# Attention on one Trainium2 core: softmax denominators inverted by ScalarE's logarithm and exponential instead of VectorE's reciprocal

## The reference

```
scores = einsum('bqhd,bkhd->bhqk', q, k) / hd + slopes * rel      # causal, else the lowest float
attn   = softmax(scores, axis=-1)
out    = einsum('bhqk,bkhd->bqhd', attn, v).reshape(B, S, H)
return out @ w_proj + b_proj
```

## Time and profile before

| | us |
|---|---|
| median of 3 runs (lowest, highest) | 1267.71 (1266.81, 1270.55) |
| the profiled execution | 1269.12 |
| its span | 1267.3 |

### The profile page before, as it was taken

The page is one execution under the profiler, slowest core; times in us unless marked ns, Lnnn a source line. Parts: engine busy times, 40 slices in busy tenths (PEclk is TensorE's granted clock), DMA queues, the critical chain, the costliest instruction groups (busy, mean ns, idle before and its releaser), DMA issues. The chain is left out here.

```text
span 1267.3 us, 31645 instructions
## 1 busy us (share of the span) xinstructions
PE 1114.0 (88%) x12161; PEld 914.5 (72%) x12161; DVE 869.7 (69%) x2188; ACT 630.5 (50%) x1433; POOL 387.9 (31%) x561
## 2 busy tenths in 40 slices
PE   6569998779979995657799999999999999999987
PEld 5446776657778994546557888888888888888776
DVE  6466997778846678767476677667766776664574
ACT  4434555331433664547644554555455545553654
POOL 3331123076710155771055016202620261000120
PEclk9769999687989998777999999999999999999998
DMA  7737885222279886462343234223343332232001
GB/s 175 187 115 208 221 226 193 100 79 84 80 262 418 320 301 225 144 178 100 112 105 98 85 111 126 85 85 114 121 152 90 117 114 88 90 102 80 1 18 50
DMA packets 77986, 176.17 MB, mean 139 GB/s; under 512 B 12614, under 2 KB 26182, under 8 KB 75270
## 3 DMA queue, kind: packets, MB, share of 16 engines
q1 hardware_dynamic: 71564, 157.09, 38.8%
q0 software_dynamic: 6272, 17.05, 4.4%
HBM read 112.82 MB, written 61.08 MB: 137 GB/s over the span
## 5 line engine op out<-in xcount | busy, mean ns | idle before, releaser
L2373 ACT ACTIVATE decay<-masked,negcum 128x128 f32<-128x128 f32 x512 | 163.0, 391 | 102.1 <-DVE mixT L2437 102.1
L2281 PE MATMUL joint<-xh,w_high 128*128 128x512 f32 x512 | 209.3, 409 | 2.2 <-POOL wl L2217 2.2
L2281 PE MATMUL joint<-xl,w_high 128*128 128x512 f32 x512 | 200.2, 391 | 0.0
L2281 PE MATMUL joint<-xh,wl 128*128 128x512 f32 x512 | 199.8, 390 | 0.0
L2485 DVE COPY cT<-joint 128x512 f32<-128x512 f32 x128 | 88.3, 690 | 85.7 <-PE joint L2281 85.4
L2391 ACT ACTIVATE bT<-joint 128x512 f32<-128x512 f32 x128 | 76.7, 599 | 130.8 <-PE joint L2281 130.8
L2437 DVE TENSOR_TENSOR mixT<-pcb,decay 128x512 f32<-128x512 f32 x128 | 82.4, 685 | 55.8 <-PE pcb L2297 55.7
L2214 POOL TENSOR_TENSOR w_high<-w_in,none 128x512 fp32r<-128x512 f32 x32 | 35.0, 1094 | 261.4 <-DMA w_in<-in_w_bc 250.8
L2281 PEld LDWEIGHTS joint<-xh,w_high 128*128 128x128 f32 x512 | 96.1, 188 | 23.9 <-POOL wl L2217 2.6
L2281 PEld LDWEIGHTS joint<-xh,wl 128*128 128x128 f32 x512 | 96.1, 188 | 20.7
L2281 PEld LDWEIGHTS joint<-xl,w_high 128*128 128x128 f32 x512 | 96.3, 188 | 17.0
(11 more groups left out here) (367 smaller groups left out, 2711.7 us busy)
## 6 DMA issues: line engine op xcount, KB each, us to landing
cumrow<-ssm_cum SPq DMA_DIRECT2D x128, 256.0 KB, 3.3
slots_in<-blank SPq DMA_DIRECT2D x16, 1024.0 KB, 5.5
rows<-slots_in SPq DMA_DIRECT2D x32, 512.0 KB, 5.3
slots_out<-spare SPq DMA_DIRECT2D x32, 512.0 KB, 3.9
weights<-in_expert_quads SPq DMA_DIRECT2D x16, 768.0 KB, 9.1
w_in<-in_w_bc SPq DMA_DIRECT2D x32, 256.0 KB, 3.7
qk_parts<-parts SPq DMA_DIRECT2D x32, 192.0 KB, 2.3
stack<-qk_parts SPq DMA_DIRECT2D x32, 192.0 KB, 5.3
```

Source lines behind the costliest of these rows:

```text
L2281: last = nc.tensor.matmul(bank[:], w[:, j, col:col + P], a[:, k, c * CHUNK:(c + 1) * CHUNK], start=(m == 0), stop=(m == len(parts) - 1))
L2373: last = nc.scalar.activation(decay[:, n % 2, o], masked[:, n % 2, o], ACT.Exp, bias=negcum[:, c * TPC + i, head:head + 1])
```

## The change

DVE's two reciprocals per unit go. ACT gets a function `invert` that takes the natural logarithm of the denominators (128x256, from PSUM to SBUF) and then the exponential of its negative in place, with a semaphore (`logged`) between the two. DVE's `normalise` waits for ACT's one signal in place of its own two.

```
@@ stage_attention
-        inverted, normed = chip.sem("inverted"), chip.sem("normed")
+        logged, inverted, normed = chip.sem("logged"), chip.sem("inverted"), chip.sem("normed")
@@ block.scalar
+                def invert(u):
+                    act.wait_ge(pv_done, u + 1)
+                    if u:
+                        act.wait_ge(normed, u)
+                    nc.scalar.activation(rinv[:], po[u % 2][:, 1, :], ACT.Ln).then_inc(logged, 1)
+                    act.wait_ge(logged, u + 1)
+                    nc.scalar.activation(rinv[:], rinv[:], ACT.Exp, scale=-1.0).then_inc(inverted, 1)
...
                         hand_over(n // HALF - 1)
+                    u = i // HALF - 2
+                    if i % HALF == AT_BLOCK and 0 <= u < UNITS:
+                        invert(u)
@@ block.vector
-                def invert(u, half):
-                    if half == 0:
-                        dve.wait_ge(pv_done, u + 1)
-                        if u:
-                            dve.wait_ge(normed, u)
-                    cols = slice(half * P, (half + 1) * P)
-                    nc.vector.reciprocal(rinv[:, cols], po[u % 2][:, 1, cols]).then_inc(inverted, 1)
-
                 def normalise(u):
-                    dve.wait_ge(inverted, 2 * u + 2)
+                    dve.wait_ge(inverted, u + 1)
...
-                        for half in range(2):
-                            invert(u, half)
                         normalise(u)
                         block_norms(u + 2)
```

## The result

The changed kernel took 1284.01 us (median of 4 runs, 1282.55 to 1285.83) against 1267.61 us for the kernel before: a ratio of 1.0138 [1.0111, 1.0164]. By the medians that is 16.4 us slower, by the ratio (which is not the quotient of the medians) 17.5 us. The forecast was 1282 us. The profiled execution of the changed kernel took 1282.55 us, span 1280.7 us.

The account below looks back on a forecast made before the run. No engine is busy throughout attention; what is late when a window ends (DVE's or ACT's path) counts. Windows 12.5 us plus one clock loss gave 14.2 us on 1267.7: 1282 us, range 1264.5 to 1291.

Parts of the forecast that it names:

- The load back to the exponential: On ACT in the attention stage: returning from logarithm to exponential needs another table load, taken as 1.28 us.
- one table serves both: Rival: ACT loads once, each inversion takes 0.88 us; net -1.6 us, 1266 us, no measurable change; chance 0.24.
- the 1.8 us at the end: In the one-table rival, the last projection of the attention stage starts 1.8 us earlier.
- The inversion of 3.48 us: Each inversion on ACT: two loads of 1.28 us, two activations of 0.42 us, four gaps of 0.02 us.
- The windows: Attention's per-unit stretches, w0 onward, from one unit's `values` to the next: late inversions lengthen them by 12.5 us in all.
- Whose path: Which engine delays the next window: DVE's late maxima in w4, w6, w10; ACT's queued scalings and exponentials in w8, w12.
- The clock: PE's granted clock falls after the longer stalls behind w8 and w12; one loss of 1.7 us counted for both.
- the rival of six falls: Late windows idle PE 1 to 2 us more; six clock losses of 1.7 us, 23 us, 1290 us; chance 0.10.
- ACT's waits for turned scores: In attention, ACT's waits for PE's turned scores shrink by some 40 us as inversions fill them.
- The end: Last two inversions on ACT end about 227.4 us, where the last reciprocal ended at 227.47: nothing gained or lost.

Follow-up runs that it names:

- loads_aside: Kernel before, DVE still inverting, plus a logarithm and exponential of a scratch tile with their loads on ACT in each window, nobody waiting: 1279.66 us, 1.0091.
- clock_fill_fit: Changed kernel plus long f32 matmuls of no use on PE in w4, w6, w8, w10 and w12, sized to fit its waits: 1278.72 us, 1.0101.
- the second profile: Profile from the first repeat of the changed kernel, no edit: 1283.40 us, 1.0142 of the kernel before.
- the third: Profile from the second repeat of the changed kernel, no edit: 1282.56 us, 1.0146 of the kernel before.

## Why the prediction was right, and where it was off

- *The load back to the exponential.* Right, and with it the whole case: one 1283 ns load in each direction. The argument was the second load in the earlier trace rows. Asking for the common set makes the rival "one table serves both" come true, near its price: 0.998 is 2.5 us less, the rival had 1.6, and it had the 1.8 us at the end right.
- *The inversion of 3.48 us.* 3.41 us; its logarithm and exponential together 0.80 us, forecast 0.84.
- *The windows.* With the clock held up, the growth is +1.13, +1.60, +2.10 and +1.22 us in w4, w6, w8 and w10 (forecast 1.2, 1.75, 2.2, 1.2), +3.43 in w12 (3.5), +0.75 in w14 (0.9), +0.83 and +0.58 in w9 and w11 (0.8 each). All within 0.22 us. w2, put at nothing, gave back 0.6 us in every profile of the changed kernel, where its clock stayed up, and w0 cost up to 0.4.
- *Whose path.* loads_aside shows it as the forecast had it: DVE's in w4, w6 and w10, ACT's in w8 and w12.
- *The clock: the term that was mis-sized.* Forecast one fall, 1.7 us. By the sums of w0 to w14 the falls took 17.0 - 11.4 = 5.6, 2.2 and 3.1 us in three executions, in two to four windows at 0.8 to 1.7 us each, and what lasted into the next; that lies between the forecast and the rival of six falls. Against more falls the forecast held that the page's line of the clock stood at its highest digit from 95 to 222 us. But one digit is a mean over 32 us: the slice that holds the stretch of 0.72 in the earlier trace rows shows that digit too, so the line could not show falls of this size. Waits of 0.41 and 0.96 us in w4 did harm in one execution of three. The windows came out 1.1 us smaller than forecast and the clock 0.5 to 3.9 us larger, so part of the nearness of the sum is luck.
- *ACT's waits for turned scores.* Forecast 40 us less, measured 29.2. The two inversions behind the last exponentials, some 7 us, take the place of no such wait, and at the low clock PE's turned scores come slower (47 waits instead of 30; 33 waits of 19.2 us in all in clock_fill_fit).
- *The end.* Right: the last projection starts 7.82 us behind w15 in all three profiles of the changed kernel, against 7.64 before. But its own length was 2.66 us before, 2.58, 3.07 and 2.50 in the changed kernel and 3.51 in clock_fill_fit, by the clock it got; so a whole-stage difference of 1 us says nothing here.

What stays open: in the first pair of profiles the stage grew by 17.1 us and the execution by 13.4; the rest of the program, which the change does not touch, was 3.7 us shorter in one than in the other. And in the second profile the stage grew by 14.2 us, while the runs of that set say 17.4 by their medians; in the third it is 14.5 against 16.1. The second profile was the fastest of its six runs (so was the third of its six), at a mean granted clock of 0.933; the slowest, 1287.82 us, had 0.929. How much of the 16 us is clock is thus known to a few us only: clock_fill_fit puts it at 1.0146 - 1.0101, or 5.7 us (3.8 us by the medians), on one chip and in one set of runs, and the two intervals meet at 1.012. Why code added in one stage made PE wait 2.6 us in a later one is not settled either; clock_fill_fit had one such wait too, of 1.06 us and at another place (788.74 us), in its profiled run, which was the slowest of its six.

## What to carry to other kernels

Before a function is moved to ScalarE, look in the trace for a table load on the way back as well as on the way there, and if two functions alternate, ask once for a set that holds both: the same 16 inversions were 1.4% slower or 0.2% faster by that line alone. Take the price of a longer queue from each window, by the path that ends last there; the engine's total of idle time (54 us here against 55 us of added work) says nothing of it. Every new wait on TensorE's path may also cost clock, so put a few falls, not one, into the range.

## What the runs showed of the hardware that was not expected

- An f32 matmul of 128x256 on PE showed as two instructions of 0.22 us each, so that fillers sized by count ran twice as long as meant. `project` shows the same: four matmuls in the kernel's loop (L666), eight in the rows.
- 165 small matmuls in one stage went with a wait of 2.4 to 2.6 us in code 700 us later, in both profiles of that kernel; with 74 and 52 instructions of long ones there was none and one of 1.06 us.
- The granted clock fell behind the same waits of 0.41 and 0.96 us in one execution and stayed up in two; behind the same wait of 2.37 us it fell in two and stayed up in one. Behind 4.34 us (w12) it fell in all three.
